# A vision layer with routed experts on one core: the embedding placed between scores and values, and four scatters of an expert under way

## The chip, the core and the metric

The kernel runs on one core of a Trainium2 chip. The metric is the time of one execution on the device in microseconds (us). The engines of the core are TensorE (PE in the profile; its weight loads are PEld), VectorE (DVE), ScalarE (ACT), GpSimd (POOL) and SyncE (SP), which here only issues transfers. Each runs its own list of instructions in order; between engines order is made by semaphores: an instruction waits until a count is reached, and a finished instruction or transfer raises one.

## The reference

128 images of 64 x 64 pixels are cut into 16 patches each, which gives 2048 tokens. All arithmetic is in float32.

```
h  = patches @ W_tok.T + b                        # 768 -> 192
# attention: 12 heads of 16, causal, 16 tokens per image, with rotary tables
q, k, v = split(layernorm(h) @ W_attn + b)
h  = h + softmax(mask(rope(q) @ rope(k).T / 4)) @ v @ W_proj + b_proj
# experts: 16, each token takes its best 4
x2 = layernorm(h);  t = rmsnorm(x2) * scale
comb = softmax over the top 4 of (t @ gate_w.T + gate_b), 0 elsewhere
y_e  = (min(g,7) * sigmoid(1.702 g) * (clip(l,-7,7) + 1)) @ mlp2_e + b2_e   # g, l: even and odd of t @ mlp1_e + b1_e
h  = h + x2 + sum_e comb_e * y_e
```

## The kernel before

**Token phase.** The tokens are 16 tiles of 128. They pass through a software pipeline of seven stages, written out by hand and unrolled: step n works on tile n in stage 0, tile n-1 in stage 1, and so on to tile n-6 in stage 6. The function `step` exists once per engine and lists what that engine does in a step, in this order; nothing else orders the work but the semaphore waits.

- Stage 0: TensorE embeds the tile (`embed`, L411, twelve matmuls of line L414), VectorE adds the bias and takes the statistics (L785 to L795), GpSimd takes the inverse root, VectorE normalises.
- Stage 1: TensorE turns the normalised tile (L420) and makes q, k (L436, L437) and v (L440, L441); VectorE applies the rotary tables, ScalarE copies v (v_sb, line L634).
- Stage 2: q and k are turned, ScalarE spreads k over heads (k_spread, L652), TensorE makes the scores (L452), VectorE masks them and subtracts the maximum, ScalarE takes the exponential (prob, L697).
- Stage 3: VectorE sums and inverts, GpSimd weighs the probabilities (p_pair, L1157), VectorE turns them (pT), ScalarE spreads them (p_spread, L634), TensorE multiplies them with v (`values`, L480), ScalarE copies the result (yT, L634).
- Stage 4: projection (`project`, L459), residual, second layer norm, root mean square (L689, L1132, L1135).
- Stage 5: t is turned, the gate product (L464, L465), the best four experts (L902 to L914).
- Stage 6: weights, ranks of the tokens within their experts, and the tile's scatter: four indirect transfers of GpSimd (`scatter`, L1144) write the 128 rows to the regions of their experts in a table in memory, `routed_rows`. The weights are turned (L432), copied by ScalarE (combT) and multiplied with the second bias (L470); VectorE adds that (L981), and SyncE stores the tile as the base of the output.

In TensorE's step the embedding comes first. It waits for two things that free its PSUM bank: h0 of the tile before has been added, and combT of the last step has been copied (both live in bank 0). It is followed by the turns, the projection, the ranks, q and k, the gate product, the scores, the values, the bias product and last the v product. In ScalarE's step the copies go xnT, qT, k_spread, tT, p_spread, combT, then the square, yT, the exponential, the experts' exponential and v_sb. In GpSimd's step p_pair comes first, then two inverse roots, the four scatters, a third root and the residual. SyncE loads the next input once the tile two before it is embedded (L340), then one expert's weights (L350, L352), then stores a base tile (L356).

**Table.** From the counts VectorE works out which expert each of 79 slots of 128 rows belongs to, where its rows begin, and how much of the scatters' semaphores it must wait for (`tab`, 22 small operations). TensorE turns three columns of it and VectorE copies them to one row, `table_i` (L1063).

**Expert phase.** The 79 slots are worked through two at a time: SyncE loads the slot's rows (`load_rows`, L388, 16 buffers), TensorE turns them (L569), ScalarE copies rows (rT) and the expert's first weights (w_now), TensorE does the first layer (L589, L597), ScalarE and VectorE the activation (L724, L1077 to L1090), TensorE the second layer (L611), VectorE weighs the result and works out the rows to which it goes (`weigh`, y_out and row_to, L1097, L1100; four buffers), and GpSimd adds it to the output with an indirect accumulating transfer (L1200).

Rows of one expert belong to different tokens, so two slots of one expert may be under way together; slots of different experts, and spare slots at the start, may not. Before a scatter GpSimd waits on two semaphores, which even and odd slots raise in turn (`added`): the scatter two slots back must always have landed, and the one just before too if the expert changes, which a number of the table says:

```python
wait(pool, added[b % 2], owed_to(j - 2, b))
owed = pool.value_load(table_i[0:1, 2, bass.ds(j, 1)], min_val=16, max_val=16 * SLOTS)
pool.wait_ge(added[(b - 1) % 2], owed)
```

Of the kernel before, what the change touches and what calls it, by code (L numbers as in the profile page):

```python
# [16 lines left out]
P = 128  # L17
# [23 lines left out]
TABLE_STEPS = 22  # L41
# [5 lines left out]
R_STAGES = 3  # L47
R_PAIRS = (SLOTS + 1) // 2
# [19 lines left out]
def shape_constants():  # L68
# [27 lines left out]
    put("owed", 16 * ((p[:, None] - 1) // 2))  # L96
# [3 lines left out]
def build(nc, x, consts, w_tok, b_tok, w_qkv, b_qkv, w_proj, nscale, w_gate, b_gate,  # L100
          w1, b1, w2, b2, out):
    routed = nc.dram_tensor("routed_rows", (SPARE + P, ROW), F32, kind="Internal").ap()
    with ExitStack() as ctx:  # L103
# [82 lines left out]
        of_tile = sb("of_tile", [P, 10])  # L186
# [3 lines left out]
        table_i = sb("table_i", [1, 3, SLOTS], I32)  # L190
# [38 lines left out]
        ps_tab, ps_valid = banks[7][0:1, 0:3 * SLOTS], banks[7][:, 256:256 + SLOTS]  # L229
# [33 lines left out]
        added = [sem("r_added0"), sem("r_added1")]  # L263
# [41 lines left out]
        def owed_to(j, buf):  # L305

            if isinstance(j, int):
                return 16 * (j // 2 + 1) if j >= 0 else 0
            return (j - buf % 2) * 8 + 16
# [13 lines left out]
        def _(sp):  # L323
# [59 lines left out]
            def load_rows(j, buf):  # L383

                wait(sp, added[buf % 2], owed_to(j - NX, buf))
                alone(sp)
                at = sp.value_load(table_i[0:1, 1, bass.ds(j, 1)], min_val=0, max_val=SPARE)
                sp.dma_start(rows[buf], routed[bass.ds(at, P), :]).then_inc(rows_in[buf], 16)  # L388
# [8 lines left out]
            for i in range(2):  # L397
                sp.wait_ge(added[i], 16 * ((SLOTS + 1 - i) // 2))
# [4 lines left out]
        def _(pe):  # L403
# [80 lines left out]
            pe.wait_ge(wtok_in, 16)  # L484

            def step(tile, seen, n):
                par = n % 2
                if tile(0) is not None:
                    t = tile(0)
                    bank_free(("h0_ready", seen(0, 1)), ("combT_ready", seen(6, 1)))  # L490

                    embed(t, par, 16 * (t // 2 + 1) if isinstance(t, int) else (t - par) * 8 + 16)
                if isinstance(tile(0), int) and tile(0) == 0:
                    pe.wait_ge(consts_in, 16)
                    pe.wait_ge(wqkv_in, 32)
                    pe.wait_ge(wsmall_in, 16 * 7)
                    pe.wait_ge(setup_pool, 3)
                    pe.wait_ge(setup_act, 2)
                    pe.wait_ge(setup_dve, 2)
# [30 lines left out]
                if tile(2) is not None:  # L530
                    bank_free(("sc1_ready", seen(2, 1)))
                    scores(tile(2))
                if tile(3) is not None:
# [14 lines left out]
            for i in range(3):  # L548
                mm(ps_tab[:, i * SLOTS:(i + 1) * SLOTS], of_tile[0:SLOTS, i:i + 1], ident[0:SLOTS, 0:SLOTS],
# [82 lines left out]
        def _(act):  # L632
# [33 lines left out]
            def step(tile, seen, n):  # L666
# [12 lines left out]
                if tile(5) is not None:  # L679
                    move(tile(5), tT[0:HALF], ps_tT, "t_turned", "gated", "tT_ready")  # L680
                if tile(3) is not None:
                    spread_probs(tile(3))
                if tile(6) is not None:
                    move(tile(6), combT[:], ps_cT, "comb_turned", "b2_done", "combT_ready")
# [80 lines left out]
        def _(dve):  # L765
# [270 lines left out]
            column = [of_tile[:, i:i + 1] for i in range(10)]  # L1036
# [22 lines left out]
            tab(20, V.scalar_tensor_tensor, column[2], column[9], 16.0, const("owed"), ALU.mult, ALU.add)  # L1059
            assert made[0] == TABLE_STEPS  # L1060
# [32 lines left out]
            def weigh(j, buf):  # L1093
                dve.wait_ge(r["experts_done"], j + 1)
                wait(dve, added[buf % 2], owed_to(j - NY, buf))
# [18 lines left out]
        def _(pool):  # L1114
# [70 lines left out]
            def r_step(tile, seen, n):  # L1185
                if tile(2) is not None:
# [4 lines left out]
                    wait(pool, added[b % 2], owed_to(j - 2, b))  # L1191
                    alone(pool)
                    if isinstance(j, int) and j < 3:
                        wait(pool, added[(b - 1) % 2], owed_to(j - 1, b - 1))
                        alone(pool)
                    else:
                        owed = pool.value_load(table_i[0:1, 2, bass.ds(j, 1)], min_val=16, max_val=16 * SLOTS)  # L1197
                        pool.wait_ge(added[(b - 1) % 2], owed)
# [3 lines left out]
                        in_=y_out[b % NY], in_offset=None, compute_op=ALU.add).then_inc(added[b % 2], 16)  # L1202
# [56 lines left out]
```

## Time and profile before

| what | us |
|---|---|
| median of 3 runs | 524.96 |
| the runs | 522.0, 524.96, 531.15 |
| the profiled execution | 521.43 |
| its span, first to last instruction | 519.6 |
| TensorE busy in the span | 437.7 (84%) |
| VectorE, ScalarE, GpSimd busy | 303.9 (58%), 311.0 (60%), 257.2 (50%) |
| token phase with embeddings in it | about 7 to 159 |
| last stages and table | to about 229 |
| expert phase | about 229 to the end |

The profile lists each instruction with its start and length, both in us, and with the idle time of its engine before it and what ended that. "issue" there means that the profile shows nothing to wait for, "remote" that a semaphore ended the wait and no instruction that just ended fits it. The ends of matmuls are modelled. A DMA_INDIRECT row of GpSimd is the time in which it writes the descriptors; the data land later. PEclk is the granted clock of TensorE as a share of 2.4 GHz.

### The profile page before, as it was taken

Reading aid. Unit: us, or ns where it says so; the run is one execution under the profiler, and the core shown is the slowest. Engines: PE = TensorE matmul, PEld = TensorE weight load, DVE = VectorE, ACT = ScalarE, POOL = GpSimd, SP = SyncE. Lnnn points to the kernel's source line nnn. Section 1 sums busy time; section 2 is a strip of 40 time slices with the busy share of each in tenths; the row PEclk is TensorE's granted clock in tenths of the full one; section 3 lists DMA queues with packets and bytes.
Section 4 is the critical chain, followed back from the end, with each engine's and each line's share of the span. In section 5 each row is a group of like instructions: output and inputs, shape, how many; then the busy total and the mean of one; then the engine's idle time right before and its main releaser. Section 6 shows DMA issues by size and latency. Waiting matters only on the chain. (4 is left out here: it accounts for less than half of the span.)

```text
span 519.6 us, 14443 instructions
## 1 busy us (share of the span) xinstructions
PE 437.7 (84%) x3867; PEld 388.2 (75%) x3868; DVE 303.9 (58%) x1048; ACT 311.0 (60%) x832; POOL 257.2 (50%) x302
## 2 busy tenths in 40 slices
PE   3788887797777758339999999999999999999970
PEld 2666765675566546229999999999999999999970
DVE  0466977878787666614555555555555555555550
ACT  1257656666665563217776767677766767777730
POOL 1124476667676666730334445345453644454443
PEclk9899999989999775559999999999999999999995
DMA  7995554555565111223333534434434443342332
GB/s 213 218 228 163 148 159 146 151 169 159 169 179 154 54 50 50 77 87 96 49 49 50 83 57 73 68 56 64 63 56 64 64 64 58 55 65 32 32 32 23
DMA packets 42107, 49.73 MB, mean 96 GB/s; under 512 B 6387, under 2 KB 33507, under 8 KB 42052
## 3 DMA queue, kind: packets, MB, share of 16 engines
q1 hardware_dynamic: 27604, 34.35, 25.2%
q0 software_dynamic: 14448, 14.72, 18.6%
q8 instruction: 25, 0.41, 0.3%
q14 instruction: 30, 0.25, 0.2%
HBM read 30.82 MB, written 18.23 MB: 94 GB/s over the span
## 5 line engine op out<-in xcount | busy, mean ns | idle before, releaser
L1200 POOL DMA_INDIRECT out_rows<-x_sb,row_to x79 | 125.9, 1593 | 161.6 <-DMA out_rows<-x_sb,row_to 78.5
L589 PE MATMUL bank<-rT,w_now 128*128 128x128 f32 x948 | 124.0, 281 | 0.3 <-ACT rT L634 0.3
L589 PEld LDWEIGHTS bank<-rT,w_now 128*128 128x128 f32 x948 | 115.1, 193 | 5.2 <-ACT rT L634 0.5
L634 ACT ACTIVATE w_now<-w_sb 128x1158 f32 x79 | 92.4, 1170 | 22.4 <-issue 17.2
L724 ACT ACTIVATE k_spread<-bank,w_now 128x128 f32<-128x128 f32 x237 | 70.1, 372 | 58.2 <-PE bank L597 52.5
L1077 DVE TENSOR_TENSOR v_sb<-bank,w_now 128x384 f32<-128x384 f32 x79 | 44.1, 558 | 85.5 <-PE bank L597 60.2
L611 PE MATMUL bank<-w_sb,p_spread 128*128 x474 | 83.9, 327 | 0.1
L1144 POOL DMA_INDIRECT routed_rows<-packet,row_i x64 | 64.7, 1012 | 24.1 <-issue 22.2
L611 PEld LDWEIGHTS bank<-w_sb,p_spread 128*128 128x128 f32 x474 | 76.1, 190 | 0.5 <-issue 0.4
L1090 DVE SCALAR_TENSOR_TENSOR p_spread<-k_spread,v_sb 128x384 f32<-128x384 f32 x79 | 44.1, 558 | 36.7 <-ACT k_spread L724 28.2
L597 PE MATMUL bank<-rT,w_now 64*128 64x128 f32 x948 | 64.2, 281 | 0.0
L597 PEld LDWEIGHTS bank<-rT,w_now 64*128 64x128 f32 x948 | 56.4, 188 | 5.1 <-issue 0.2
L414 PE MATMUL bank<-wtok_sb,x_sb 128*128 128x192 f32 x192 | 38.2, 354 | 10.5 <-DMA wtok_sb<-w_tok 6.8
L414 PEld LDWEIGHTS bank<-wtok_sb,x_sb 128*128 128x128 f32 x192 | 35.8, 211 | 10.5 <-DMA wtok_sb<-w_tok 6.5
L652 ACT ACTIVATE k_spread<-bank,cst 96x256 f32<-96x256 f32 x96 | 36.5, 482 | 0.0
L634 ACT ACTIVATE p_spread<-pT 32x384 f32<-32x384 f32 x64 | 33.2, 518 | 2.4 <-DVE pT L865 1.7
L1100 DVE TENSOR_SCALAR x_sb<-bank,row_w 128x192 f32<-128x192 f32 x79 | 31.8, 410 | 0.0
L634 ACT ACTIVATE rT<-bank 128x256 f32<-128x256 f32 x79 | 26.2, 381 | 9.3 <-PE bank L569 8.6
L1082 DVE TENSOR_SCALAR v_sb<-v_sb 128x384 f32<-128x384 f32 x79 | 29.9, 379 | 2.8
L634 ACT ACTIVATE yT<-bank 128x384 f32<-128x384 f32 x16 | 7.9, 491 | 39.2 <-remote 36.4
L459 PE MATMUL bank<-wproj_sb,yT 128*128 128x192 f32 x96 | 23.3, 388 | 9.5 <-issue 9.3
L459 PEld LDWEIGHTS bank<-wproj_sb,yT 128*128 128x128 f32 x96 | 18.5, 224 | 12.7 <-issue 12.7
(182 smaller groups left out, 598.8 us busy)
## 6 DMA issues: line engine op xcount, KB each, us to landing
x_sb<-patches SPq DMA_DIRECT2D x16, 384.0 KB, 3.6
w_sb<-w SPq DMA_DIRECT2D x32, 192.0 KB
w_sb<-w SPq DMA_DIRECT2D x16, 288.0 KB
w_sb<-w SPq DMA_DIRECT2D x64, 48.0 KB
wtok_sb<-routed_rows SPq DMA_DIRECT2D x25, 106.0 KB, 2.0
routed_rows<-zero_row SPq DMA_DIRECT2D x17, 106.0 KB
out_rows<-h SPq DMA_DIRECT2D x16, 96.0 KB
out_rows<-x_sb,row_to POOLq DMA_INDIRECT x79
```

The lines of the kernel that those rows point to most:

```text
L414: last = mm(ps_e, x_sb[buf][:, c, :], wtok_sb[:, c, :], start=(c == 0), stop=(c == PCH - 1))
L459: last = mm(ps_p, yT[:, c, :], wproj_sb[:, c, :], start=(c == 0), stop=(c == YCH - 1))
L589: last = mm(dst[:, c * P:(c + 1) * P], w[:, a:a + P], t[:, part, :], start=(start and c == 0), stop=(not start and c == ICH - 1))
L597: last = mm(dst[:, c * P:(c + 1) * P], w[k:k + half, REST + c * P:REST + (c + 1) * P], t[k:k + half, 1 - part, :], start=(start and c == 0 ...
L611: last = mm(ps_yo[buf % 2], act_sb[buf % 4][:, c, :], w2_sb[:, bass.ds(expert, 1), c, :].rearrange("p a f -> p (a f)"), start=(c == 0), st ...
L634: return nc.scalar.activation(dst, src, ACT.Copy)
L652: last = nc.scalar.activation(k_spread[:, :, :, h], ps_kT.rearrange("p c (j i k) -> p c j i k", j=PAIRS, i=2), ACT.Copy, scale=const("head ...
L724: last = nc.scalar.activation(gate_act[b][:, a:a + P], ps_glu[b][:, a:a + P], ACT.Silu, bias=w1_now[b][:, GLU_B + c:GLU_B + c + 1], scale= ...
L1077: V.tensor_tensor(lin[b].rearrange("p (c t) -> p c t", c=ICH), ps_lin[b][:, 0:INNER].rearrange("p (c t) -> p c t", c=ICH), w1_now[b][:, LI ...
L1090: V.scalar_tensor_tensor(act_sb[buf % 4].rearrange("p c t -> p (c t)"), gate_act[b], SILU_LIMIT, lin[b], ALU.min, ALU.mult).then_inc(r["ac ...
L1144: G.indirect_dma_start(out=routed, out_offset=bass.IndirectOffsetOnAxis(ap=row_i[buf][:, k:k + 1].bitcast(U32), axis=0), in_=packet[buf][: ...
L1200: G.indirect_dma_start(out=out, out_offset=bass.IndirectOffsetOnAxis(ap=row_to[:, b % NY:b % NY + 1].bitcast(U32), axis=0), in_=y_out[b % ...
```

## The change

Two things change, and they do not touch each other.

In the token phase TensorE embeds tile 0 before the first step, and in step n it embeds tile n+1, between the scores of tile n-2 and the values of tile n-3. Its waits are moved along: h0 of tile n and combT of this step. For that ScalarE copies combT before it spreads the probabilities, where before it did so behind them.

In the expert phase four semaphores are raised in turn (`ADDS = 4`) in place of two. A scatter waits for the three before it only as far as the table says: to the end of them where the expert changes or the slot is spare, and otherwise only for those that share a semaphore with them, four slots earlier. The scatter four back is waited for by VectorE, before it writes over that slot's y_out. The table has one column more (with one operation of `tab` and one small matmul more), since the three semaphores can owe two different counts. SyncE's load of a slot's rows waits until the slot sixteen back has been weighed, where before it waited until that slot's scatter had landed.

```diff
-TABLE_STEPS = 22
+TABLE_STEPS = 23
+ADDS = 4
...
-    put("owed", 16 * ((p[:, None] - 1) // 2))
+    put("owed", 16 * (p[:, None] // ADDS))
...
-        ps_tab, ps_valid = banks[7][0:1, 0:3 * SLOTS], banks[7][:, 256:256 + SLOTS]
+        ps_tab, ps_valid = banks[7][0:1, 0:4 * SLOTS], banks[7][:, 384:384 + SLOTS]
...
-        added = [sem("r_added0"), sem("r_added1")]
+        added = [sem(f"r_added{i}") for i in range(ADDS)]
...
-                return 16 * (j // 2 + 1) if j >= 0 else 0
-            return (j - buf % 2) * 8 + 16
+                return 16 * (j // ADDS + 1) if j >= 0 else 0
+            return (j - buf % ADDS) * (16 // ADDS) + 16
...
             def load_rows(j, buf):
-                wait(sp, added[buf % 2], owed_to(j - NX, buf))
+                wait(sp, r["y_out_ready"], j - NX + 1)
...
             pe.wait_ge(wtok_in, 16)
+            embed(0, 0, 16)
+            (the waits for constants and weights)
             def step(tile, seen, n):
-                par = n % 2
-                if tile(0) is not None:
-                    t = tile(0)
-                    bank_free(("h0_ready", seen(0, 1)), ("combT_ready", seen(6, 1)))
-                    embed(t, par, 16 * (t // 2 + 1) if isinstance(t, int) else (t - par) * 8 + 16)
-                (the waits for constants and weights, at tile 0)
...
                     scores(tile(2))
+                if n + 1 < TILES:
+                    bank_free(("h0_ready", n + 1), ("combT_ready", seen(6)))
+                    embed(n + 1, (n + 1) % 2, 16 * ((n + 1) // 2 + 1))
                 if tile(3) is not None:
...
-            for i in range(3):
+            for i, a in enumerate((0, 1, 2, 10)):
...
                     move(tile(5), tT[0:HALF], ps_tT, "t_turned", "gated", "tT_ready")
+                if tile(6) is not None:
+                    move(tile(6), combT[:], ps_cT, "comb_turned", "b2_done", "combT_ready")
                 if tile(3) is not None:
                     spread_probs(tile(3))
-                if tile(6) is not None:
-                    move(tile(6), combT[:], ps_cT, "comb_turned", "b2_done", "combT_ready")
...
+            tab(22, V.tensor_scalar, column[10], column[2], -16.0, None, ALU.add)
...
             def weigh(j, buf):
-                wait(dve, added[buf % 2], owed_to(j - NY, buf))
+                wait(dve, added[buf % ADDS], owed_to(j - NY, buf))
...
-                    wait(pool, added[b % 2], owed_to(j - 2, b))
                     alone(pool)
-                    if isinstance(j, int) and j < 3:
-                        wait(pool, added[(b - 1) % 2], owed_to(j - 1, b - 1))
+                    if isinstance(j, int) and j < 2 * ADDS:
+                        for i in range(1, ADDS):
+                            wait(pool, added[(j - i) % ADDS], owed_to(j - i, (j - i) % ADDS))
                         alone(pool)
                     else:
-                        owed = pool.value_load(table_i[0:1, 2, bass.ds(j, 1)], min_val=16, max_val=16 * SLOTS)
-                        pool.wait_ge(added[(b - 1) % 2], owed)
+                        if b % ADDS > 0:
+                            owed = pool.value_load(table_i[0:1, 2, bass.ds(j, 1)], min_val=32, max_val=16 * SLOTS)
+                        if b % ADDS < ADDS - 1:
+                            owed_wrap = pool.value_load(table_i[0:1, 3, bass.ds(j, 1)], min_val=16, max_val=16 * SLOTS)
+                        for i in range(1, ADDS):
+                            pool.wait_ge(added[(b - i) % ADDS], owed if b % ADDS >= i else owed_wrap)
                         alone(pool)
...
-                        in_=y_out[b % NY], in_offset=None, compute_op=ALU.add).then_inc(added[b % 2], 16)
+                        in_=y_out[b % NY], in_offset=None, compute_op=ALU.add).then_inc(added[b % ADDS], 16)
```

## Rows read from the trace of the kernel before

**Rows 1.** Windows of all engines, expert phase; columns: stretch, busy us (and instructions) per engine, PEclk, DMA share, GB/s.

```profile
230.00:504.00 274.00, 271.96 (x2528) 260.86 (x2528) 149.62 (x395) 190.60 (x474) 120.45 (x76) 0.99 0.39 59
```

**Rows 2.** Waits of TensorE, 231 to 504: us in total, times, longest.

```profile
PE bank L569 <- DMA wtok_sb<-routed_rows: 4.6, 2, 4.2
```

**Rows 3.** Timeline of TensorE, steps 3 to 5; columns: start, us, what, idle before it.

```profile
35.17 0.86 PE L480 MATMUL bank<-p_spread,v_sb 128*32 128x128 f32 x24 [1.01 <-ACT p_spread L634]
...
36.72 2.11 PE L414 MATMUL bank<-wtok_sb,x_sb 128*128 128x192 f32 x12
...
44.02 0.86 PE L480 MATMUL bank<-p_spread,v_sb 128*32 128x128 f32 x24 [1.11 <-ACT p_spread L634]
...
53.14 0.86 PE L480 MATMUL bank<-p_spread,v_sb 128*32 128x128 f32 x24 [0.58 <-ACT p_spread L634]
```

**Rows 4.** Timeline of GpSimd, first scatter of a tile, five of the token steps.

```profile
62.26 1.20 POOL L1144 DMA_INDIRECT routed_rows<-packet,row_i  x1 [0.89 <-issue]
...
130.99 1.07 POOL L1144 DMA_INDIRECT routed_rows<-packet,row_i  x1 [0.73 <-issue]
...
143.47 1.07 POOL L1144 DMA_INDIRECT routed_rows<-packet,row_i  x1 [0.73 <-issue]
...
154.23 1.07 POOL L1144 DMA_INDIRECT routed_rows<-packet,row_i  x1 [0.73 <-issue]
...
167.04 1.07 POOL L1144 DMA_INDIRECT routed_rows<-packet,row_i  x1 [0.73 <-issue]
```

**Rows 5.** Timeline of TensorE and ScalarE, steps 12 and 13.

```profile
131.64 0.86 PE L480 MATMUL bank<-p_spread,v_sb 128*32 128x128 f32 x24 [0.58 <-ACT p_spread L634]
...
136.03 0.49 ACT L634 ACTIVATE yT<-bank 128x384 f32<-128x384 f32 x1 [3.76 <-remote]
...
143.42 0.86 PE L480 MATMUL bank<-p_spread,v_sb 128*32 128x128 f32 x24 [1.05 <-ACT p_spread L634]
...
145.16 0.49 PE L441 MATMUL bank<-wqkv_sb,xnT 97*128 97x192 f32 x2
...
147.01 0.49 ACT L634 ACTIVATE yT<-bank 128x384 f32<-128x384 f32 x1 [2.57 <-remote]
...
149.27 0.33 ACT L634 ACTIVATE v_sb<-bank 128x192 f32<-128x192 f32 x1 [1.33 <-remote]
```

**Rows 6.** Timeline of GpSimd, p_pair of step 13.

```profile
138.56 1.10 POOL L1157 TENSOR_TENSOR p_pair<-prob,rinv_own 128x192 f32<-128x192 f32 x2 [0.94 <-DVE rinv_own L857]
```

**Rows 7.** Timeline, between the token steps and the expert phase.

```profile
226.79 0.40 DVE L1063 CAST table_i<-bank 1x237 int32<-1x237 f32 x1 [3.27 <-issue]
...
229.10 2.58 SPq L388 DMA_DIRECT2D wtok_sb<-routed_rows  x3
```

**Rows 8.** Timeline of GpSimd, scatters of the expert phase, early and last.

```profile
282.23 1.56 POOL L1200 DMA_INDIRECT out_rows<-x_sb,row_to  x1 [2.63 <-DVE x_sb L1100]
...
284.09 1.56 POOL L1200 DMA_INDIRECT out_rows<-x_sb,row_to  x1 [0.30 <-issue]
...
287.26 1.81 POOL L1200 DMA_INDIRECT out_rows<-x_sb,row_to  x1 [1.61 <-DMA out_rows<-x_sb,row_to]
...
499.82 1.64 POOL L1200 DMA_INDIRECT out_rows<-x_sb,row_to  x1 [0.32 <-issue]
...
503.19 1.56 POOL L1200 DMA_INDIRECT out_rows<-x_sb,row_to  x1 [1.73 <-DMA out_rows<-x_sb,row_to]
...
507.44 1.56 POOL L1200 DMA_INDIRECT out_rows<-x_sb,row_to  x1 [2.68 <-DMA out_rows<-x_sb,row_to]
...
512.43 1.56 POOL L1200 DMA_INDIRECT out_rows<-x_sb,row_to  x1 [1.57 <-DMA out_rows<-x_sb,row_to]
```

**Rows 9.** Windows, and timeline of TensorE, step 16 and step 13.

```profile
169.00:178.00 9.00, 6.23 (x22) 4.25 (x21) 5.50 (x24) 6.18 (x19) 5.43 (x10) 0.62 0.14 49
...
173.14 2.26 PE L459 MATMUL bank<-wproj_sb,yT 128*128 128x192 f32 x6 [1.21 <-issue]
...
137.65 1.14 PE L459 MATMUL bank<-wproj_sb,yT 128*128 128x192 f32 x6
```

More of the change, by code:

```diff
@@ L185, in build @@
         passed, jump, jumped = sb("passed", [P, EXPERTS]), sb("jump", [P, EXPERTS]), sb("jumped", [P, EXPERTS])
-        of_tile = sb("of_tile", [P, 10])
+        of_tile = sb("of_tile", [P, 11])
         ends_at = sb("ends_at", [P, EXPERTS])
@@ L189, in build @@
         pad_to = sb("pad_to", [P, SLOTS], I32)
-        table_i = sb("table_i", [1, 3, SLOTS], I32)
+        table_i = sb("table_i", [1, 4, SLOTS], I32)
         ones_f = sb("ones_f", [P, EXPERTS])
@@ L396, in _ @@
                 load_rows(j, j % NX)
-            for i in range(2):
-                sp.wait_ge(added[i], 16 * ((SLOTS + 1 - i) // 2))
+            for i in range(ADDS):
+                sp.wait_ge(added[i], 16 * ((SLOTS + ADDS - 1 - i) // ADDS))
             sp.wait_ge(base_out, 16 * TILES)
@@ L484, in _ @@
             pe.wait_ge(wtok_in, 16)
-            def step(tile, seen, n):
-                par = n % 2
-                if tile(0) is not None:
-                    t = tile(0)
-                    bank_free(("h0_ready", seen(0, 1)), ("combT_ready", seen(6, 1)))
-                    embed(t, par, 16 * (t // 2 + 1) if isinstance(t, int) else (t - par) * 8 + 16)
[L493 to L499, printed above, removed]
+            embed(0, 0, 16)
+            pe.wait_ge(consts_in, 16)
+            pe.wait_ge(wqkv_in, 32)
+            pe.wait_ge(wsmall_in, 16 * 7)
+            pe.wait_ge(setup_pool, 3)
+            pe.wait_ge(setup_act, 2)
+            pe.wait_ge(setup_dve, 2)
+            def step(tile, seen, n):
                 if tile(1) is not None:
@@ L547, in _ @@
             pe.wait_ge(table_step, TABLE_STEPS)
-            for i in range(3):
-                mm(ps_tab[:, i * SLOTS:(i + 1) * SLOTS], of_tile[0:SLOTS, i:i + 1], ident[0:SLOTS, 0:SLOTS],
+            for i, a in enumerate((0, 1, 2, 10)):
+                mm(ps_tab[:, i * SLOTS:(i + 1) * SLOTS], of_tile[0:SLOTS, a:a + 1], ident[0:SLOTS, 0:SLOTS],
                    start=True, stop=True)
@@ L1034, in tab @@
                 made[0] += 1
-            column = [of_tile[:, i:i + 1] for i in range(10)]
+            column = [of_tile[:, i:i + 1] for i in range(11)]
             dve.wait_ge(counted, 1)
```

## The prediction

> **What bounds the kernel now.** I read three views, in this order. First the busy time of the engines by stage. The 274 us from 230 to 504, the expert phase, hold 271.96 us of TensorE work at 0.99 of the full clock [rows 1], and in them TensorE waited 4.6 us for its own rows, twice, both at the start [rows 2]. So TensorE is the bound there; GpSimd's scatters run beside it, and only those behind the last matmul can set the end.
>
> Second, the timeline of TensorE in the token steps. In the steps before any scatter it stands idle just ahead of the values product: 1.01, 1.11 and 0.58 us in steps 3, 4 and 5, for the copy of the probabilities, and the embedding, 2.11 us, comes after the values and the v product, with no gap [rows 3]. These steps go at TensorE's pace.
>
> Third, GpSimd in the steps from 6 on, where each tile's four scatters go out. I call the start of the first of them S. Nine steps lie between S = 62.26 and S = 167.04 [rows 4]: 104.78 us, 11.64 each. They are of two kinds. From S = 130.99 to the next is 12.48 us, from 143.47 to the next 10.76, from 154.23 to the next 12.81. Four are long (12.02 to 12.81) and five short (10.76 to 11.88). What separates them is when ScalarE begins to copy yT, which needs the signal of the values product [rows 5]. The signal comes late: the values end at 132.50 and the copy starts at 136.03, after 3.76 us of idleness whose releaser the profile can only call remote; in the next step they end at 144.28 and the copy starts at 147.01. Counted from S, the values end at 1.51 and 0.81, and the copies start at 5.04 and 3.54. All nine steps sort the same way: where the values end 0.56 to 0.85 after S, the copy starts 2.9 to 4.3 after S (five steps); where they end 1.37 to 1.57 after S, it starts 5.0 to 5.8 after S (four steps), which are the four long ones. The v product of the short step ends at 145.65, S + 2.18, and its copy starts at 149.27, S + 5.80. So a signal of TensorE that falls among the scatters is seen when they are nearly over, and one that just precedes them is seen sooner. A late yT copy makes the exponential behind it on ScalarE late, then the sums on VectorE, and GpSimd's p_pair waits 0.94 us for them [rows 6]; everything that GpSimd has queued behind p_pair, the next S too, moves with it.
>
> **The change, part by part.** *Embedding before the values, steps 3 to 5.* Nothing is added; 2.11 us of work moves into gaps of 1.01, 1.11 and 0.58 [rows 3]. Between scores and values it covers each whole gap: -2.7 us together. The values then start 2.11 less the gap later, and yT and the exponential after them; the transposed probabilities reach ScalarE behind its key copies, which gives them room. Step 2 has no values, so nothing there. Ends: 0 (the exponential becomes the next wait) and -2.7. I take -2.7, because the rows show ScalarE and not VectorE as the releaser.
>
> *The same in the nine steps with scatters.* The gap ahead of the values is 0.58 or 1.05 us [rows 5], so they end 1.53 or 1.06 us later: at about S + 3.0 instead of 1.51 and S + 1.9 instead of 0.81. Both now lie past 1.37, where every signal in this trace was seen at S + 5.0 or later. What TensorE saves at the head of the next step buys nothing, since there it waits for that yT and v anyway. So all nine steps become long ones. At 12.48 each: 112.3 us against 104.78, +7.5. Ends: 12.02 each gives +3.4, 12.81 each gives +10.5; I take 12.48, whose step has the middle of the four delays.
>
> The Trainium skill, "TensorE: Matmul & The Clock Gate", section Part 3: Packing small matmuls, says that matmuls start and end strictly in issue order. That speaks against this edit: the values' signal cannot overtake the twelve matmuls put before them. No row here shows matmuls out of order; by this rule alone, with signals seen at once, the cost would be the shift and no more.
>
> *ScalarE copies combT before the probabilities.* The embedding writes its bank, so it needs that copy first. It is a 16 x 128 copy and bounded from above by the 0.49 us of the 128 x 384 one [rows 5]. It delays the probabilities, which now have the embedding's 2.11 us as cover: 0. Without that cover it would be up to 0.49 x 9 = 4.4.
>
> *SyncE's queue.* Input loads wait for the previous embedding, so they may go out earlier, but behind the same expert loads and base stores of that queue; TensorE waits for an input only at tile 1, which keeps its place. 0.
>
> *Table.* One VectorE operation more, one small matmul more, a longer copy. The table's copy starts at 226.79 and takes 0.40; the first row load, which waits also for the last token scatter to land, goes out at 229.10 [rows 7], 1.9 us after the copy. That slack covers them. 0, at most +0.6, the length of three such operations.
>
> *Row loads wait for the weighed output, not for the scatter.* They go out earlier; TensorE does not wait for rows after the start [rows 2]. 0.
>
> *Four scatters.* A scatter that depends on the one before starts 4.25 us behind it (503.19 to 507.44), an independent one 1.86 behind, and where two are under way a start waits 5.03 for the one two before (282.23 to 287.26) [rows 8]. All but the last few hide beside TensorE. The last expert change is at 507.44; the slot of 503.19 could go at 499.82 + 1.86 = 501.7, its successor at 501.7 + 5.0 = 506.7, and the last two at 508.6 and 510.4 instead of 512.43. That is -2.0, less about 0.5 because three then share the transfer: -1.5. Ends: 0 (the three stretch each other as much as they gained) and -2.8 (no stretch). The second table read per slot runs in GpSimd's sequencer during the 1.55 us of the scatter before: 0.
>
> The Trainium skill, "DMA: Bandwidth & Descriptors", section Anatomy of one DMA, gives about 2.0 us per transfer plus bytes over 436 GB/s, nearly all of it completion latency. By it, transfers under way do not stretch each other and the end comes 2.8 us earlier; the 5.03 against 4.25 speaks against that, and I go by the rows.
>
> Sum: -2.7 + 7.5 - 1.5 = +3.3 on the profiled execution's 521.43 us (span 519.6): 524.7, rounded to 525. The three runs shown lie at 522.0, 524.96 and 531.15; the profiled one is below them all. I keep its basis and let the range take the 3.5 us to the median.
>
> **Rivals.** *A, the signal's delay is set by the scatters and not by the values' end.* Then the nine steps stay as they are: -2.7 - 1.5 = -4.2, 517.2. For it: releases fall close to ends of scatters. Against: the sorting above, nine of nine, and the v signal.
>
> *B, what holds the signals is TensorE's own stream behind them,* the embedding that follows. Then with the embedding ahead all nine steps are short: 9 x 10.76 = 96.8, -7.9, and with the rest -12.1: 509.3. For it: the embedding is the longest stretch of matmuls behind the signal. Against: in steps 4 and 5 it also follows the values, and no such delay is seen.
>
> *C, slower beyond the forecast: the granted clock.* Now the embedding stands where TensorE would idle, from v product to the next turns. With it gone, idle time at each step's head grows by 2.11 us. After such idle time, from 169 on, when tiles to embed have run out, the granted clock is 0.62 in the mean, the lower of its levels (1.2 GHz) for part of it, and the projection takes 2.26 us [rows 9] against 1.14 at the full one. At 1.12 more in nine steps this adds 10.1: 534.8. It decides if the clock falls at the head of steps 7 to 14.
>
> *D, the change does not do what it says at the end:* expert changes or stretching keep the last scatters where they are. 526.2.
>
> **Numbers.** Forecast 0.43, A 0.25, B 0.13, C 0.13, D 0.06. From no change a measurement of this kernel tells about 2%, 10.4 us: under 511.0 or over 531.9. Faster: most of B and a little of A, 0.14. Slower: C and the top of the forecast's own band, 0.15. Same: 0.71. The forecast's own band is 518 to 530; the range reaches to A below and nearly to C above, with 3.5 us for the median: 512 to 533, which leaves out B and most of C, 0.2.
>
> **What would show it.** Right: idle time of 0.58 to 1.1 ahead of the values gone, yT copies at S + 5.0 to 5.8 in every step, S to S 12 to 12.8, first S about 2.7 earlier, last scatter 0 to 3 us behind where it was relative to the last matmul. Wrong: yT copies at S + 3.5 or less in most steps (B), an unchanged alternation (A), the granted clock under 0.9 between 70 and 160 (C), or an expert phase that is not 274 us long, which no part of this foresees.

## The result, and the profile after

The changed kernel takes 529.33 us in the median (525.45 to 532.45), the kernel before 525.11 on the same chips (520.23 to 531.15): a ratio of 1.0099, 95% interval 1.0076 to 1.0121. The interval leaves out 1.000: the change costs about 1%, too little for the 2% that the prediction wanted before it called the change slower. (Ratios leave out the few executions that ran longer at a lower clock.) The profiled execution has a span of 526.0 us against 519.6, +6.4.

The windows of all engines, token steps with scatters, then the expert phase (columns as in [rows 1]):

```profile
62.00:168.00 106.00, 86.38 (x680) 64.63 (x672) 73.47 (x315) 56.87 (x176) 68.37 (x110) 0.89 0.51 148
...
240.00:512.00 272.00, 271.01 (x2526) 259.98 (x2526) 151.01 (x393) 190.06 (x473) 119.18 (x76) 0.99 0.39 59
```

The expert phase is as before [rows 1]: TensorE busy all the time, from 239.79 to 512.6, 272.8 us long against 272.7. So the loss lies ahead of it. The timeline of TensorE in steps 3 to 5 after:

```profile
33.67 2.22 PE L415 MATMUL bank<-wtok_sb,x_sb 128*128 128x192 f32 x12
35.82 0.86 PE L481 MATMUL bank<-p_spread,v_sb 128*32 128x128 f32 x24
...
43.69 0.86 PE L481 MATMUL bank<-p_spread,v_sb 128*32 128x128 f32 x24
...
52.34 0.86 PE L481 MATMUL bank<-p_spread,v_sb 128*32 128x128 f32 x24
```

The idle times of 1.01, 1.11 and 0.58 us ahead of the values [rows 3] are gone. Then come the steps with scatters. Timeline after: the first and the last S of the nine periods, and one whole step, S = 136.95:

```profile
60.47 1.20 POOL L1143 DMA_INDIRECT routed_rows<-packet,row_i  x1 [0.89 <-issue]
...
136.56 2.22 PE L415 MATMUL bank<-wtok_sb,x_sb 128*128 128x192 f32 x12
136.95 1.07 POOL L1143 DMA_INDIRECT routed_rows<-packet,row_i  x1 [0.73 <-issue]
...
138.71 0.86 PE L481 MATMUL bank<-p_spread,v_sb 128*32 128x128 f32 x24
139.50 0.59 PE L471 MATMUL bank<-b_sb,combT 16*128 16x192 f32 x2
...
140.85 0.96 POOL L1143 DMA_INDIRECT routed_rows<-packet,row_i  x1 [0.30 <-issue]
142.80 0.49 ACT L632 ACTIVATE yT<-bank 128x384 f32<-128x384 f32 x1 [4.52 <-remote]
142.85 0.35 DVE L979 TENSOR_TENSOR h<-h,bank 128x192 f32<-128x192 f32 x1 [3.14 <-remote]
143.30 0.61 PE L421 MATMUL bank<-cst,qk 128*96 128x128 f32 x4 [2.14 <-issue]
144.05 1.97 PE L460 MATMUL bank<-wproj_sb,yT 128*128 128x192 f32 x6
144.92 1.22 POOL L1156 TENSOR_TENSOR p_pair<-prob,rinv_own 128x192 f32<-128x192 f32 x2 [1.63 <-DVE rinv_own L855]
...
174.82 1.07 POOL L1143 DMA_INDIRECT routed_rows<-packet,row_i  x1 [0.73 <-issue]
```

From 60.47 to 174.82 are 114.35 us, 12.7 each, against 104.78 [rows 4]. The values end at S + 2.62 and yT is copied at S + 5.85, where a short step of before had S + 3.54 [rows 5]. So it is in eight of the nine steps (5.76 to 6.05); the first, at S + 3.6, is the exception. In one of the eight, S = 72.25, no signal is late: TensorE ran at 0.50 of its clock from 70 to 74, the embedding took 3.09 us, the values ended only at S + 5.92, and the copy followed 0.13 us later. In the other seven the values ended at S + 1.6 to 3.7. Two things follow from late signals here, and the prediction followed only one: yT, exponential, sums, p_pair (1.63 us late); and the b2 product's signal, which VectorE's bias addition (L979) sees at S + 5.90, after which TensorE may turn q and k (2.14 us idle), because the bank that holds the b2 product is the one it turns q into.

At the end, the last scatters of the expert phase after, GpSimd:

```profile
515.05 1.56 POOL L1203 DMA_INDIRECT out_rows<-x_sb,row_to  x1 [2.73 <-DMA out_rows<-x_sb,row_to]
516.91 1.56 POOL L1203 DMA_INDIRECT out_rows<-x_sb,row_to  x1 [0.30 <-issue]
518.77 1.56 POOL L1203 DMA_INDIRECT out_rows<-x_sb,row_to  x1 [0.30 <-DMA out_rows<-x_sb,row_to]
```

The last starts 6.2 us behind the last matmul (512.6), before it was 8.6 (512.43 and 503.86): -2.4. Between token steps and experts, after:

```profile
229.97 0.21 DVE L1031 SCALAR_TENSOR_TENSOR of_tile<-of_tile,cnt,cst 128x1 f32<-128x1 f32 x1
230.10 0.15 DVE L1031 TENSOR_TENSOR of_tile<-of_tile,passed 128x1 f32<-128x1 f32 x1
...
232.03 0.16 DVE L1031 SCALAR_TENSOR_TENSOR of_tile<-of_tile 128x1 f32<-128x1 f32 x1 [1.79 <-remote]
...
236.14 0.48 DVE L1062 CAST table_i<-bank 1x316 int32<-1x316 f32 x1 [2.62 <-PE bank L549]
...
237.77 4.75 SPq L389 DMA_DIRECT2D wtok_sb<-routed_rows  x5
```

The last token scatter is at 232.51, so the row loads start 5.3 us behind it against 3.5 before (225.59 and 229.10 [rows 7]). Here the table is the later one, by 1.8. One wait in it deserves a second reading. The operation at 232.03 waits for a semaphore that only VectorE raises, and for the one at 229.97, which ended at 230.18: among the last scatters VectorE started 1.85 us after the operation of its own that it waits for. Whether the signal was late or VectorE itself was held, the rows do not tell. The sum of the trace: S of step 15 +7.8 (-1.8 at the first S, +9.6 over nine periods), the rest of the token steps -0.9, table +1.8, end -2.4, and 0.1 elsewhere: +6.4.

### The profile page after: what moved, and what is told of

It is laid out like the page before. It is cut to its first block and busy times, and to the rows that moved or that the text cites. A ratio compares the mean times of both kernels' runs of the same rounds, so it can differ in the third digit from the quotient of the medians.

```text
span 526.0 us, 14562 instructions
## 1 busy us (share of the span) xinstructions
PE 449.3 (85%) x3869; PEld 394.2 (75%) x3870; DVE 304.5 (58%) x1049; ACT 309.0 (59%) x832; POOL 255.0 (48%) x302
## 5 line engine op out<-in xcount | busy, mean ns | idle before, releaser
L1203 POOL DMA_INDIRECT out_rows<-x_sb,row_to x79 | 124.2, 1572 | 162.7 <-DMA out_rows<-x_sb,row_to 60.4
L415 PE MATMUL bank<-wtok_sb,x_sb 128*128 128x192 f32 x192 | 40.2, 365 | 9.2 <-DMA wtok_sb<-w_tok 5.8
L415 PEld LDWEIGHTS bank<-wtok_sb,x_sb 128*128 128x128 f32 x192 | 35.3, 212 | 13.9 <-issue 8.1
L1081 DVE TENSOR_SCALAR v_sb<-v_sb 128x384 f32<-128x384 f32 x79 | 31.7, 402 | 2.7
L1156 POOL TENSOR_TENSOR p_pair<-prob,rinv_own 128x192 f32<-128x192 f32 x32 | 17.9, 581 | 31.0 <-DVE rinv_own L855 31.0
L460 PE MATMUL bank<-wproj_sb,yT 128*128 128x192 f32 x96 | 27.4, 440 | 4.9 <-issue 4.3
```

The costliest lines, as they stand in the source:

```text
L415: last = mm(ps_e, x_sb[buf][:, c, :], wtok_sb[:, c, :], start=(c == 0), stop=(c == PCH - 1))
L1203: G.indirect_dma_start(out=out, out_offset=bass.IndirectOffsetOnAxis(ap=row_to[:, b % NY:b % NY + 1].bitcast(U32), axis=0), in_=y_out[b % ...
```

## The experiments

All ratios are to the kernel before, run beside it. "Nine periods" is from the first S to the tenth. The edits are shown shortened.

**One part at a time.** The scatter part alone leaves TensorE's and ScalarE's order as it was:

```diff
+ADDS = 4        # with its table entry, waits and row loads; embed(t) stays first in step()
```

> The scatter part of the change alone on the kernel before: four scatters of an expert under way, with their table entries and the earlier row loads; the embedding stays first in its step. Theory (values' signal falls among the scatters): token steps as before, nine periods 104.8 us, end term -2, table not late since the token steps are not: 523 us against 525, ratio 0.996. Rival (the table's extra entry costs about 1.8 us wherever it stands): 525, ratio 1.000.

Measured 0.9983 (0.9955 to 1.0012); nine periods 104.0. At the end the last scatter is at 512.52 and the last matmul at 506.3, 6.2 apart, 2.4 less than before. Of these 2.4 us, 0.9 show in the ratio. Its interval holds both the 0.996 of the theory and the 1.000 of the rival; what speaks against the rival is the start of the row loads, 3.7 us behind the last token scatter against 3.5 before.

```diff
+                if n + 1 < TILES:
+                    embed(n + 1, ...)          # between scores and values; combT before probs
                 values(tile(3), (n - 3) % 2)   # two scatters under way, as before
```

> The embedding part alone on the kernel before: embedding between scores and values, ScalarE's combT copy ahead of the probabilities; two scatters under way as before. Theory: the whole loss of the change and the loss of its end gain, 525 + 6.4 + 2.3 = 533 to 534, ratio 1.015 to 1.018; yT copies at S + 5.8 in nearly every step. Rival A (scatters alone set the delay): 522, ratio 0.995.

Measured 1.0118 (1.0077 to 1.0159); nine periods 112.9, yT at S + 5.7 to 5.8 in eight of them. The product of the two parts is 1.0101, the whole change 1.0099: the parts add up, and the loss is the embedding's. It is less than the 1.015 expected, though its interval reaches there. The table's 1.8 us does not come with this part (row loads 3.5 us behind the last scatter), which would account for the difference; that is argued and not shown.

**Is it where the values end?** The values run twice, and nothing else moves:

```diff
-                for h in range(HEADS):
+                for h in list(range(HEADS)) * (2 if t >= 3 else 1):
```

> The kernel before; in steps 6 to 18 TensorE runs the 24 values matmuls twice (same operands, same results), 0.86 us more before their signal. Embedding, queues and order stay, and TensorE's head of the step stays full. Theory (the values' end relative to the first scatter sets when the copy of yT starts): values end at S + 1.4 to 2.4, copies at S + 5.0 to 5.8 in nearly every step, nine periods 112 us against 105, clock as before: 531, ratio 1.012. Rival A (scatters alone set it): alternation as before, at most +1: ratio 1.000. Rival C (it is the clock): also 1.000, since no idle time is added at the head.

Measured 1.0296 (1.0248 to 1.0344). The timeline of one step:

```profile
90.43 1.07 POOL L1144 DMA_INDIRECT routed_rows<-packet,row_i  x1 [0.73 <-issue]
...
92.49 0.39 PE L480 MATMUL bank<-p_spread,v_sb 128*32 128x128 f32 x2 [0.34 <-issue]
...
96.37 0.49 ACT L634 ACTIVATE yT<-bank 128x384 f32<-128x384 f32 x1 [4.97 <-remote]
96.41 0.35 DVE L981 TENSOR_TENSOR h<-h,bank 128x192 f32<-128x192 f32 x1 [3.22 <-remote]
```

Values end at S + 2.4 here, and yT is copied at S + 5.94; in all nine steps it is 5.94 to 6.04, with the embedding at its old place. The first seven periods are 12.87 each, as after, at a granted clock of 0.98 over the seven. That rules out rival A as it was stated, an unchanged alternation, and the clock as the cause of these seven. The last two are 13.9 and 16.1, which no theory had, and which bring the ratio beyond the 1.012: in them TensorE's embedding takes 3.64 and 4.05 us instead of 2.11, the first at a granted clock of 0.60 (160 to 164). So doubling the values costs a second thing, and the ratio is no measure of the first.

**Is it the clock (rival C)?** The granted clock did fall, from 0.98 to 0.89, and the projection of the step above took 1.97 us. The head of the step is filled with repeated transposes:

```diff
-                for c in range(2):
+                for c in [0, 1] * (6 if dst is ps_xT and t >= 5 else 1):
```

> The kernel after; from step 6 on TensorE turns the normalised tile (tile 1 of the step) six times over instead of once, about 2 us of transposes at the head of the step where the embedding stood before, ahead of the same signal. Rival C: the granted clock between 62 and 170 goes back from 0.88 to 0.96 or more, the slow projections (2.0 to 2.3 us) go, and the time falls to 521 to 524, ratio 0.993 to 0.998 of before. Theory: the clock goes back but the nine periods stay at 12.7, since ScalarE and VectorE wait for signals until S + 5.8 whatever the clock: 529, ratio 1.010.

Measured 1.0083 (1.0053 to 1.0113). The windows from first S to tenth, of the kernel after and of this one:

```profile
60.47:174.82 114.35, 93.87 (x741) 70.41 (x739) 81.10 (x352) 63.12 (x197) 72.89 (x117) 0.88 0.50 146
```

```profile
61.04:174.95 113.91, 96.05 (x836) 75.11 (x834) 81.64 (x352) 63.20 (x197) 71.68 (x117) 0.97 0.51 147
```

The clock is back (0.88 to 0.97), though two of the nine projections still take 2.1 us, and the nine periods are not (114.35 to 113.91). The lower clock accompanies the loss and does not make it: TensorE has slack while it waits for the late signals.

**Is it the values' signal alone?** The embedding goes directly behind the values, so that these end as early as before and only what follows is later:

```diff
                     values(tile(3), (n - 3) % 2)
+                if n + 1 < TILES:
+                    embed(n + 1, ...)
                 if tile(6) is not None:
                     experts_bias(tile(6))
```

> The kernel before with the embedding of the next tile directly behind the values product instead of first in the next step; everything else as before. The head of the step is as empty of TensorE work as in the kernel after, but the values end as early after S as in the kernel before. Theory (what counts is where the values end after the first scatter): short and long steps alternate as before, 105 us for nine, 525 us, ratio 0.995 to 1.005. Rival C (the empty head lowers the granted clock and that costs the time): as slow as the embedding part alone, 533, ratio 1.015, with the granted clock at 0.88 between 62 and 170. Rival B (the embedding behind the signal holds it): no faster than before either, so this run does not bear it out or down alone.

Measured 1.0113 (1.0070 to 1.0156): my theory's 0.995 to 1.005 fell. The step at S = 87.43:

```profile
87.43 1.07 POOL L1141 DMA_INDIRECT routed_rows<-packet,row_i  x1 [0.73 <-issue]
...
90.31 0.59 PE L470 MATMUL bank<-b_sb,combT 16*128 16x192 f32 x2
...
91.01 0.49 ACT L631 ACTIVATE yT<-bank 128x384 f32<-128x384 f32 x1 [2.61 <-remote]
...
93.28 0.35 DVE L978 TENSOR_TENSOR h<-h,bank 128x192 f32<-128x192 f32 x1 [3.09 <-remote]
93.55 0.35 DVE L845 TENSOR_REDUCE rsum<-prob 128x12 f32<-128x192 f32 x1
...
93.73 0.61 PE L420 MATMUL bank<-cst,qk 128*96 128x128 f32 x4 [1.76 <-issue]
...
94.89 1.10 POOL L1154 TENSOR_TENSOR p_pair<-prob,rinv_own 128x192 f32<-128x192 f32 x2 [1.11 <-DVE rinv_own L854]
```

The values' signal is seen early (yT at S + 3.58, and at 3.5 to 4.3 in eight of the nine steps, though the embedding runs right behind it, which goes against rival B). But b2 now ends at S + 3.47, its signal is seen at S + 5.85, and two things are queued behind the bias addition: the sums of the next step on VectorE, hence p_pair, and TensorE's turns. Nine periods of 12.4. The clock is 0.95, so C does not explain it either. The theory that I took on from here: the signals of TensorE that fall among the scatters are late, and the step is as long as the last of those that something waits for. It is a rule for the values, b2 and v products and not for every signal. In the kernel after, in the step at S = 72.25, the gate product ended at S + 0.68 and VectorE began to read it at S + 0.78; the scores ended at S + 2.12 and were read at S + 2.31.

**Can the late signals be got out of the way?** ScalarE's exponential goes ahead of yT, VectorE's sums ahead of the bias addition:

```diff
-                move(tile(3), yT[:], ps_yT, "pv_done", "proj_done", "yT_ready")
                 nc.scalar.activation(prob[:], sc2[:], ACT.Exp)...
+                move(tile(3), yT[:], ps_yT, "pv_done", "proj_done", "yT_ready")
...
+                at(2, prob_sum); at(2, prob_inverse); at(2, prob_inverse_own)
                     at(6, add_bias)
```

> The kernel after, with what waits for TensorE's late signals put behind what does not: ScalarE computes the exponential ahead of the copy of yT, and VectorE sums and inverts the probabilities at the end of the step, ahead of the bias addition, not first in the next step. Theory (the loss is the exponential and the sums queued behind yT and the bias): GpSimd's p_pair starts at S + 6.3 without idle time, nine periods 10.8 to 11.3 us, 97 to 102 us: 515 to 519, ratio 0.984 to 0.992, though yT is still copied at S + 5.8. Rival (the late yT itself, through the projection, sets the period): 12.7 us each as before, ratio 1.010.

> The same reordering on ScalarE and VectorE, and four scatters of an expert under way, but with the embedding first in its step as in the kernel before. Theory: nine periods of 10.8, 97 us against 105, end term -2: 514 to 516, ratio 0.980 to 0.986, within 0.5% of the one with the embedding ahead of the values. Rival: as the scatter part alone, ratio 0.998.

Measured 1.0010 (0.9977 to 1.0042) on the kernel after, 0.9969 (0.9942 to 0.9996) with the embedding first in the step. Both theories missed; they had at most 0.992 and 0.986. The reordered kernel after, step at S = 85.21:

```profile
85.21 1.07 POOL L1143 DMA_INDIRECT routed_rows<-packet,row_i  x1 [0.73 <-issue]
...
91.05 0.49 ACT L632 ACTIVATE yT<-bank 128x384 f32<-128x384 f32 x1 [3.16 <-remote]
91.10 0.35 DVE L979 TENSOR_TENSOR h<-h,bank 128x192 f32<-128x192 f32 x1 [2.34 <-remote]
91.53 0.97 POOL L1156 TENSOR_TENSOR p_pair<-prob,rinv_own 128x192 f32<-128x192 f32 x2
91.55 0.61 PE L421 MATMUL bank<-cst,qk 128*96 128x128 f32 x4 [2.29 <-issue]
```

p_pair waits for nothing now, as expected, and yet the period is 12.3, not 10.8. TensorE's turns still stand behind the bias addition at S + 5.9, and the projection behind yT. The chain through p_pair that the prediction followed is thus worth 0.4 us of a period.

The run with the embedding first shows what the bias addition does alone. Its step at S = 147.11:

```profile
147.05 0.86 PE L481 MATMUL bank<-p_spread,v_sb 128*32 128x128 f32 x24 [0.83 <-ACT p_spread L635]
147.11 1.07 POOL L1146 DMA_INDIRECT routed_rows<-packet,row_i  x1 [0.73 <-issue]
147.85 0.59 PE L471 MATMUL bank<-b_sb,combT 16*128 16x192 f32 x2
...
151.49 0.49 ACT L635 ACTIVATE yT<-bank 128x384 f32<-128x384 f32 x1 [1.70 <-remote]
...
152.92 0.35 DVE L982 TENSOR_TENSOR h<-h,bank 128x192 f32<-128x192 f32 x1 [2.26 <-remote]
...
153.41 0.97 POOL L1159 TENSOR_TENSOR p_pair<-prob,rinv_own 128x192 f32<-128x192 f32 x2
```

yT is copied at S + 4.4, p_pair waits for nothing, and only the bias addition is late, at S + 5.8. Four of its nine steps are like this and last 11.9 to 12.1 us; the two in which the bias addition also comes early (S + 3.6 and 4.4) last 10.9 and 11.1. So this chain alone costs about 1 us of a period. Its nine periods are 106.1, against 104.0 of the scatter part without the reordering: b2 ends at S + 1.33 in this step as in one of that run, and is seen at 5.8 here and at 4.3 there. The end of a product does not fix when its signal is seen.

**The embedding where no scatter goes out.**

```diff
-                if n + 1 < TILES:
+                if n < 6:            # embed ahead of values in steps 0 to 5
...                                   # from step 7 on embed(n) first in the step again
```

> The kernel after, but the embedding stands between scores and values only in steps 0 to 5, in which no token scatter goes out; from step 7 on it is first in its step again, with ScalarE's order as before. Theory: the 2.7 (after: 1.8) us of the early steps are kept, nine periods about 105 us as before, end term -2.3: 525 - 4.1 = 521, ratio 0.992. Rival (the early steps' gain is given back when the first scatters come): 523, ratio 0.996.

Measured 0.9945 (0.9910 to 0.9980), between the theory's 0.992 and the rival's 0.996, and its interval holds both. Nine periods are 107.0 and not 105. In two of them TensorE's embedding, at the head again, takes 3.94 and 4.05 us instead of 2.11 (granted clock 0.50 from 146 to 152), and those periods are 12.6 and 12.4, though yT is copied at S + 4.3 and 3.6. A low clock can make a step long too, where the embedding has no slack.

```diff
+                    experts_bias(tile(6)); v_product(tile(1))   # ahead of values
                     values(tile(3), (n - 3) % 2)
```

> The kernel with the embedding ahead of the values in steps 0 to 5 only and four scatters of an expert under way; ScalarE copies combT ahead of the probabilities, and TensorE does the b2 and v products (1.45 us) between scores and values, in place of the gap of 0.6 to 1.05 us. Theory: b2's and v's signals precede the first scatter and are seen at once, so the bias is not late; the values end 0.4 to 0.9 us later, S + 1.3 to 1.7, so that yT is copied at S + 4.3 to 5.0 in most steps and at 5.8 in some; nine periods 103 to 108 us: ratio 0.990 to 1.000. Rival (only the last signal of a step matters): the last signal now ends at S + 1.5 instead of S + 2.2 and all periods are short, 98 us, ratio 0.981.

Measured 1.0091 (1.0048 to 1.0135); both theories missed. Its profiled execution ran at a granted clock of 0.83 (62 to 160), so I read only the order of things, in the step at S = 99.06: b2 ends at S + 0.35, the bias addition is at S + 2.7, but the values end at S + 2.0 and yT is copied at S + 5.86. One late signal that is waited for is enough. (In three other steps the values themselves end only at S + 5.4, and those periods are 14.2 to 14.5.)

**Are the scatters what holds the signals?** The four scatters of a tile stay, but GpSimd does its mean root and residual between the second and the third:

```diff
-                    scatter(tile(6), (n - 6) % 2)
+                    scatter(tile(6), (n - 6) % 2, range(2))
                     inverse_root(... "rms_ready"); residual(tile(4))
+                    scatter(tile(6), (n - 6) % 2, range(2, TOPK))
```

> The kernel after, with the token scatters of a tile in two pairs: two, then GpSimd's mean root and residual (about 1.4 us), then the other two. The computation is the same. Theory (signals of TensorE that fall among back-to-back scatters are seen only when the group is nearly over, here at S + 5.8): after two scatters the signals of values, b2 and v are seen at about S + 2.9 to 3.5, and the exponential and sums are in time for p_pair: nine periods 11 to 11.8 us against 12.7, 516 to 523, ratio 0.985 to 0.997 of before. Rival (the signals are late because of the embedding's stream, or of TensorE's clock): yT still at S + 5.8, 529, ratio 1.010. Other rival: yT early, but the second pair holds the signals of the next turns instead, and the period stays over 12.3.

> The kernel with the embedding ahead of the values in steps 0 to 5 only, four scatters of an expert under way, and the token scatters in two pairs as in the run above. Theory: with the values ending at S + 0.8, all signals are seen by S + 3.5: nine periods at GpSimd's pace of 10.8 to 11.2, 98 to 101 us: 513 to 517, ratio 0.978 to 0.986. Rival (second pair holds the turns' signals): as without the split, ratio 0.9945.

> The kernel before, untouched but for the token scatters of a tile in two pairs, with GpSimd's mean root and residual between them. Theory (the held signals are a cost of the back-to-back scatters, in the kernel before too): all signals seen by S + 3.8, nine periods of 10.4 to 10.9, 94 to 98 us against 105: 515 to 519, ratio 0.980 to 0.988. If the ratio is above that of the kernel after with the same split (0.9635), the moved embedding and the four scatters are worth the difference once no signal is held. Rival (the split pays only with the moved embedding): ratio 0.995 to 1.005.

Measured 0.9635 (0.9593 to 0.9678) on the kernel after, 0.9747 (0.9692 to 0.9803) with the early embedding, 0.9823 (0.9775 to 0.9870) on the kernel before. The first, 505.1 us, beats both kernels; its span is 500.7. It gained more than the theory's 0.985, the second is a little below the 0.978 to 0.986 expected, the third is inside its range. Timeline of the kernel after with pairs, step at S = 91.59, and its nine periods as a window:

```profile
91.59 1.07 POOL L1143 DMA_INDIRECT routed_rows<-packet,row_i  x1 [0.73 <-issue]
...
92.14 0.86 PE L481 MATMUL bank<-p_spread,v_sb 128*32 128x128 f32 x24
...
92.96 0.96 POOL L1143 DMA_INDIRECT routed_rows<-packet,row_i  x1 [0.30 <-issue]
...
94.57 0.49 ACT L632 ACTIVATE yT<-bank 128x384 f32<-128x384 f32 x1 [2.00 <-remote]
94.61 0.35 DVE L979 TENSOR_TENSOR h<-h,bank 128x192 f32<-128x192 f32 x1 [0.26 <-PE bank L471]
...
95.79 1.07 POOL L1143 DMA_INDIRECT routed_rows<-packet,row_i  x1 [0.18 <-issue]
...
60.00:154.00 94.00, 85.05 (x743) 62.24 (x741) 79.72 (x352) 64.66 (x199) 72.87 (x117) 1.00 0.60 178
```

The second scatter ends at S + 2.3 and everything that TensorE signalled is seen at S + 3.0 (values and b2); with four back to back the last ends at S + 4.9 and it is S + 5.9. The same scatters, the same work, and the release moves with the end of the unbroken run of them. The nine periods are 94.0, 10.4 each, GpSimd's own pace. Neither the embedding's stream nor the clock does that: in all nine steps of all three runs with pairs yT is copied at S + 2.9 to 3.0, with the embedding ahead of the values or at the head, at a granted clock of 1.00, 0.90 or 0.88. The pairs also let GpSimd do its root and residual over 2 us earlier. What that alone is worth no run tells apart; a step of before in which p_pair waits for nothing is 10.76 long, so the last 0.36 us down to 10.4 is not the late signals' doing.

And the moved embedding, a loss of 1% before, is now a gain: 0.9635 against 0.9823, of which the four scatters are 0.9983. On one chip, with four scatters in both, the pairs give 0.9635 with the embedding ahead of the values in every step and 0.9747 with it there in the early steps only (nine periods 94.0 and 99.1). With the embedding at the head and pairs of scatters, TensorE becomes the bound in some steps. The kernel before with pairs, S = 82.25:

```profile
86.00:90.00 4.00, 4.00 (x21) 3.96 (x20) 2.17 (x12) 1.04 (x4) 3.30 (x5) 0.67 0.27 83
...
86.12 3.36 PE L414 MATMUL bank<-wtok_sb,x_sb 128*128 128x192 f32 x12
```

The granted clock is 0.50 from 84 to 86 and 0.67 from 86 to 90; the embedding takes 3.36 us instead of 2.11 and that period is 12.35, as are two others (12.68, 12.45); the remaining six are 10.4 to 10.9. Here the clock does cost time, since no slack covers it. With the embedding in the gap the granted clock is 1.00 in the mean of the nine periods.

## Why the prediction was right, and where it was off

525.0 was predicted with a range of 512 to 533, and no change that can be told from noise as the likeliest; the ratio is 1.0099 and the median 529.3. The direction was right and the size was short: +3.3 us forecast, +4.2 between the medians, +6.4 between the two profiled executions. Most of the way from 525.0 to 529.3 is the base, an execution of 521.4 where the kernel before has a median of 525.1. The time alone does not bear out the mechanism, since the range holds rival A's 517.2 as well; the rows have to. Against the trace, the terms were off by +0.9 (steps 3 to 5), +2.1 (nine steps), -0.9 (the rest of the token steps, no term of its own), +1.8 (table) and -0.9 (end), which partly cancel. That the time came inside is partly luck.

- **What bounds the kernel, expert phase:** right, 272.8 against 272.7 us.
- **Steps 3 to 5, -2.7:** the gaps went. The first S came 1.8 earlier (2.4 in the embedding part alone), but the scatter part, whose early steps are those of before, has it 1.9 later, so one execution does not tell the size. All traces together do: the first S is at 59.8 to 62.4 in the eight runs with the embedding ahead of the values in steps 3 to 5 (mean 60.9) and at 61.4 to 64.9 in the six without (mean 63.4), -2.5.
- **Nine steps, +7.5:** right in kind, 2.1 too small: it measured +9.6. yT was copied past S + 5.0 in eight of the nine, but at 5.8 to 6.05 and not at the 5.04 of the step whose 12.48 I took; 12.7 it was. The cause was only part of it: I followed yT and the exponential to p_pair. Taking that wait away on the kernel after changed the nine periods from 114.35 to 110.9 only. The bias addition behind b2's signal, with TensorE's turns behind it, holds a step at 11.9 to 12.1 by itself (the reordered run with the embedding first); in the run with the embedding behind the values it makes the sums late too, and a period is 12.4 without a late yT.
- **The sorting by where the values end:** good for the kernel before, confirmed in direction by the doubled values. Not a rule: the first step after has values at S + 1.67 and yT at S + 3.6, while a later one (S = 98.03) has the same S + 1.67 and yT at S + 5.8, and with scatters in pairs values at S + 1.4 are seen at S + 3.0.
- **Table, 0 to +0.6:** failed by itself, +1.8. I took the slack of 1.9 us as fixed. VectorE's chain runs among the last scatters, and in one place an operation started 1.85 us after the one of VectorE itself that it waits for. Neither part alone has the delay. With the four columns the copy of the table starts 1.6 us behind the last scatter even in the scatter part alone, against 1.2 before, so the added entry had taken some of the slack.
- **Four scatters, -1.5:** -2.4, between my value and the end of -2.8. In all nine traces with four under way the last scatter starts 6.1 to 6.3 us behind the last matmul, in the five with two 8.0 to 8.8. The ratio of the part alone shows 0.9 us of it.
- **Rivals:** A as stated was ruled out by the doubled values, though half of it was right: the pairs show that the scatters do set the release. B was ruled out by the embedding right behind the values, C as a cause by the filled head, D by the end's -2.4. C's premise held (0.88 to 0.89), and its price did not: it costed a slower projection without asking what slack covers it.

The Trainium skill, "Advanced Engine Details and Errata", section Network/Comms, puts a write from one engine's sequencer to another's memory at under 100 ns. An estimate by that page would have the yT copy of the step shown at S + 2.7, and it is at S + 5.85. Other signals of this case lie near the page's figure even among the scatters: ScalarE's to VectorE behind prob was seen within 0.03 us, the gate product's of the step at S = 72.25 after 0.10.

## What to carry to other kernels

When an engine's idle time ends on a releaser the profile can only call remote, look for what GpSimd issues just then, check in the code who raises the semaphore, and count every consumer of a signal in that stretch, not only the first. Break a run of indirect DMAs with other GpSimd work before moving work on the engines whose signals it holds: here it turned a move that cost 1% into part of a gain of 3.7%. A granted clock that falls costs nothing where the engine has slack and full price where it has none, so price it by what waits for the slow instruction.

## What the runs showed of the hardware

The signals of the values, b2 and v products that fall among back-to-back indirect scatters are mostly seen late, and in steps: 2.8 to 2.9, 3.5, 4.3, 5.0 and 5.8 us after the first scatter's start in the kernel before, in the nine steps read. With the same scatters in pairs they are seen at 2.9 to 3.0. Not every signal is held. ScalarE's to VectorE (prob to rsum) is seen at once in the same stretch (147.40 and 0.36 long, then 147.79), a gate product that ended at S + 0.56 is seen at S + 0.67 (kernel before, S = 178.19), and scores that ended at S + 1.44 are read at S + 2.77 in one run (the embedding in the early steps only, S = 179.40) and others that ended at S + 1.46 at S + 1.53 in another (the embedding part alone, S = 172.75). Beside the last scatters VectorE went on only 1.85 us after an operation of its own, so TensorE's signals may not be the only ones concerned. What holds them, what sets the step in which they are seen, and why a signal at S + 1.67 was once seen at S + 3.6, stays open.

The same matmuls were granted different clocks by where they stood. With pairs of scatters it was 1.00 with the embedding in the gap and 0.88 with it at the head; with four back to back it was the other way round, 0.88 in the gap and 0.98 at the head. Why is open too.
